# Sixteen sequences through four conditioned layers: modulation's columns at other places, softplus with Exp, Ln and a minimum, and the last attention with two score pairs and two weight buffers

## What is computed

```python
def _ssm(u, Wdbc, Wdt, bdt, Alog, Dp):            # E = 512, N = 16 states, R = 64
    dbc = einsum('bse,re->bsr', u, Wdbc)
    dlt, Bm, Cm = split(dbc, [R, R + N], axis=-1)
    delta = softplus(einsum('bsr,er->bse', dlt, Wdt) + bdt)
    dA = exp(delta[..., None] * -exp(Alog))
    dBu = delta[..., None] * Bm[:, :, None, :] * u[..., None]
    h = dA_t * h + dBu_t;  y = einsum('ben,bn->be', h, C_t)     # for each of 256 tokens
    return ys + u * Dp
# layer 0: shift, scale, gate = split(silu(c) @ Wada.T + bada)
#   xs = ln(x) * (1 + scale) + shift;  skip = xs;  xs = ln(xs)
#   mz = xs @ Wz + bz;  act_mx = silu(xs @ Wx + bx)
#   y = act_mx * ssm(mz @ Wc1, ...) + act_mx * flip(ssm(flip(mz @ Wc2), ...))
#   x = x + gate * (y @ Wf + bf + skip)
# layer 1: tokens permuted; xm, z = h @ W_in; causal convolution of 4, silu, the same state recurrence, * silu(z)
# layer 2: q, k, v for 16 heads of 16; att = softmax(q k^T) v; ln, modulation, silu, projection
# layer 3: q softmaxed over features, k over tokens, y = q (k^T v); ln, modulation, silu, projection
```

## Time and profile before

| | |
|---|---|
| median of 3 runs | 3309.78 us (3307.33 to 3313.04) |
| profiled execution, its own time | 3308.65 us |
| its span | 3306.9 us |
| mean granted TensorE clock | 0.979 of full speed |
| PE / weight load | 3026.8 / 2529.6 us busy |
| ACT / DVE / POOL | 2872.9 / 2686.5 / 2661.3 us busy |

### The profile page before, as it was taken

One profiled execution on the slowest core, in us unless ns is written; L12 is line 12 of the kernel. 1 busy time (PEld: TensorE's weight loads), 2 busy tenths in 40 slices (PEclk: granted clock), 3 DMA queues, 4 the chain that ended last, 5 costly groups with the idle time before them and its releaser, 6 DMA issues.

```text
span 3306.9 us, 63710 instructions
## 1 busy us (share of the span) xinstructions
PE 3026.8 (92%) x21772; PEld 2529.6 (76%) x21772; DVE 2686.5 (81%) x3433; ACT 2872.9 (87%) x6598; POOL 2661.3 (80%) x3086
## 2 busy tenths in 40 slices
PE   7768788999999999999999999999999999988886
PEld 4656667888887888888787888888788877777754
DVE  1577788979798988979798988979898988877752
ACT  2778879899999999999999999999999989887843
POOL 0596999989898988988898898989898888767720
PEclk8799999999999999999999999999999999999988
DMA  5122222222222222222222222222222121212200
GB/s 201 42 71 63 72 80 74 83 65 84 67 85 69 73 81 68 86 65 84 69 81 71 71 85 64 86 67 84 67 81 75 64 83 63 70 54 65 61 14 9
DMA packets 133873, 239.58 MB, mean 72 GB/s; under 512 B 15374, under 2 KB 31054, under 8 KB 133296
## 3 DMA queue, kind: packets, MB, share of 16 engines
q1 hardware_dynamic: 133552, 235.50, 23.1%
HBM read 230.36 MB, written 5.08 MB: 71 GB/s over the span
## 4 chain that ended last, share of the span: by engine, by line
PE 59%; ACT 13%; DVE 13%; issue 4%; POOL 4%; DVEq 0%; POOLq 0%; ACTq 0%
PE ps_b L697 13%; PE ps_y L725 12%; DVE hst L805 7%; PE ps_v L904 6%; ACT decay L764 5%; PE ps_x L1463 4%; PE ps_x L910 4%; POOL g L820 3%; PE ps_x L1437 3%; ACT dbut L775 2%; PE ps_x L904 2%; PE ps_v L955 2%; PE ps_v L910 2%; PE ps_x L1473 2%; POOL dbut L785 1%
## 5 line engine op out<-in xcount | busy, mean ns | idle before, releaser
L820 POOL TENSOR_TENSOR g<-hst,c_bc 128x512 f32<-128x512 f32 x1536 | 1980.3, 1290 | 405.9 <-PE ps_y L725 351.4
L805 DVE TENSOR_TENSOR_SCAN hst<-decay,ps_b 128x512 f32<-128x512 f32 x1536 | 1819.8, 1208 | 307.6 <-PE ps_b L697 160.3
L764 ACT ACTIVATE decay<-delta,acoef 128x256 f32<-128x256 f32 x3072 | 1377.7, 498 | 23.0 <-DVE hst L805 21.8
L697 PE MATMUL ps_b<-ident,dbut 128*128 128x128 f32 x6144 | 937.8, 276 | 158.4 <-DVE hst L805 71.9
L725 PE MATMUL ps_y<-ident,g 128*128 128x128 f32 x6144 | 936.5, 275 | 15.8 <-ACT u L1119 12.4
L697 PEld LDWEIGHTS ps_b<-ident,dbut 128*128 128x128 f32 x6144 | 702.2, 142 | 235.6 <-issue 133.0
L785 POOL TENSOR_SCALAR dbut<-dut,bcm 128x256 f32<-128x256 f32 x1536 | 753.5, 491 | 97.1 <-ACT dut L1018 97.1
L725 PEld LDWEIGHTS ps_y<-ident,g 128*128 128x128 f32 x6144 | 725.9, 141 | 138.1 <-issue 59.2
L775 ACT ACTIVATE dbut<-dut,bcm 128x256 f32<-128x256 f32 x1536 | 766.4, 500 | 30.3 <-PE ps_b L697 28.2
L1518 ACT ACTIVATE pT<-ps_x 128x1024 f32<-128x1024 f32 x120 | 121.5, 1012 | 39.5 <-PE ps_x L1473 26.9
L1546 DVE TENSOR_REDUCE mxt<-ps_x 128x4 f32<-128x1024 f32 x120 | 144.5, 1204 | 8.7 <-PE ps_x L1437 8.7
(11 more groups left out here) (257 smaller groups left out, 3711.5 us busy)
## 6 DMA issues: line engine op xcount, KB each, us to landing
...
```

What stands on the lines that cost most here:

```text
L697: last = nc.tensor.matmul(ps_b[:, u % 2, e * T + t * P:e * T + (t + 1) * P], dbut[:, u % NDBU, t, e * P:(e + 1) * P], ident[:, :], is_tran ...
L764: last = nc.scalar.activation(decay[:, u % (DA_AHEAD + 2), e, :], delta[slot(b, s)][:, eb, :], ACT.Exp, scale=acoef[:, s, eb, n:n + 1])
L805: nc.vector.tensor_tensor_scan(line(hst[:, u % NHST, :, :].rearrange("p e t -> p (e t)")), line(decay[:, u % (DA_AHEAD + 2), :, :].rearran ...
L820: nc.gpsimd.tensor_tensor(g[:, u % NG, :, :], hst[:, u % NHST, :, :], c_bc[:, k % NCB * CHUNK + n % CHUNK, :].unsqueeze(1) .broadcast_to([ ...
```

## The change

1. `ada` gets other places, (64, 65, 94.5, 106.182 to 106.955) for PE and 111 for DVE, after `BASE[0]` = 112: three pieces within the first sequence's scans, nine in the hole at ticks 218 and 219 where the first sequence's last scans and the second's first meet. What needs its columns in stage 1 (`l1_in` and others) moves a few ticks.
2. Softplus: Abs is gone, Exp reads PSUM; Ln(1 + Exp) as before; DVE takes max(min(that, 44), value). So each half has one ACT instruction less, six for a sequence, and the pieces of `prep` on ACT are 10 in place of 12.
3. `ps_y` becomes the first bank of `ps_v`, which has three; the other two keep their use.
4. `Attention` has lists `pairs` and `weights`. `late` has the pairs `ps_b` and `ps_v`, and the weights `pT` and two buffers of `g`; score group g waits for g - 2, and Exp for g - 2.
5. Pieces of the steady part and of the special stages get new places. In the start, prep1, mx and silu of the first sequence, formerly spread over ticks 107 to 123, are at ticks 122 and 123.

```diff
+LN_TOP = 44.0
...
-Attention = namedtuple("Attention", "pair pv xt q k v y")
+Attention = namedtuple("Attention", "pairs weights pv xt q k v y")
...
     "prep1": {
-        "PE": (46, 48, 66, 69, 78, 92, 95, 96),
-        "ACT": (61, 67, 72, 72, 76, 79, 80, 80, 95, 95, 95, 96),
+        "PE": (46, 48, 66, 69, 78, 92, 94, 95),
+        "ACT": (61, 67, 72, 76, 79, 80, 92.875, 94, 94.875, 95),
         "DVE": (78, 82, 90),
...
         "prep1": {
-            "PE": (107, 107, 111.25, 112, 117, 120, 122, 123),
-            "ACT": (112, 114, 114.333, 114.5, 114.667, 117.5, 117.75, 118, 120.667, 121, 122, 123),
-            "DVE": (116, 119, 120),
+            "PE": (111, 112, 122.091, 122.273, 122.455, 122.818, 122.909, 123),
+            "ACT": (122, 122.071, 122.143, 122.214, 122.357, 122.429, 122.714, 122.786, 122.857, 123),
+            "DVE": (123, 123, 123),
...
         "ada": {
-            "PE": (-112.824, -112.765, -112.647, -112.529, -112.471, -112.412, -112.353, -112.294, -112.235, -112.118, -112.059, -112),
-            "DVE": (-5.6,),
+            "PE": (64, 65, 94.5, 106.182, 106.227, 106.455, 106.591, 106.636, 106.773, 106.818, 106.864, 106.955),
+            "DVE": (111,),
         },
...
         "l2_tail": {
-            "PE": (24, 28, 28, 29),
+            "PE": (24, 27, 27, 28),
...
         ps_b = ps("ps_b", [P, 2, 512])
-        ps_y = ps("ps_y", [P, TB, HALF * P])
-        ps_v = ps("ps_v", [P, 2, 512])
+        ps_v = ps("ps_v", [P, 3, 512])
+        ps_y = ps_v[:, 0, :].rearrange("p (t n) -> p t n", t=TB)
         ps_x = ps("ps_x", [P, 3, 512])
-        A, B_ = 0, 1
+        A, B_ = 1, 2
...
                 d = delta[i][:, 2 * k:2 * k + 2, :]
-                ch.done(nc.scalar.activation(d, bank(ps_v, v, 2), ACT.Abs))
-                yield next(at)
                 logexp()
-                ch.done(nc.scalar.activation(d, d, ACT.Exp, scale=-1.0))
+                ch.done(nc.scalar.activation(d, bank(ps_v, v, 2), ACT.Exp))
...
-                nc.vector.scalar_tensor_tensor(out=d, in0=bank(ps_v, v, 2), scalar=0.0, in1=d, op0=ALU.max,
-                                               op1=ALU.add).then_inc(S[f"dt_read_{s}"], 1)
+                nc.vector.scalar_tensor_tensor(out=d, in0=d, scalar=LN_TOP, in1=bank(ps_v, v, 2), op0=ALU.min,
+                                               op1=ALU.max).then_inc(S[f"dt_read_{s}"], 1)
...
-                else:
-                    pe.wait_ge(S["s_max"], nth("s_max", b, g_))
+                elif g_ >= len(a.pairs):
+                    pe.wait_ge(S["s_max"], nth("s_max", b, g_ - len(a.pairs) + 1))
+                pair = a.pairs[g_ % len(a.pairs)]
...
-                    else:
-                        pe.wait_ge(S["p_ready"], nth("p_ready", b, g_))
+                    elif g_ >= len(a.pairs):
+                        pe.wait_ge(S["p_ready"], nth("p_ready", b, g_ - len(a.pairs) + 1))
...
-                if g_ >= 1:
-                    act.wait_ge(S["o_full_2"], nth("o_full_2", b, g_))
+                if g_ >= len(a.weights):
+                    act.wait_ge(S["o_full_2"], nth("o_full_2", b, g_ - len(a.weights) + 1))
...
-        usual = Attention(ps_x, (ps_x, 2), xt_x, qT, kT, v2, yv)
-        late = Attention(ps_b, (ps_v, B_), dbut[:, 0, :, :], decay[:, 0:2, :, :].rearrange("p a e t -> p (a e) t"),
+        usual = Attention([ps_x], [pT[:, :, :, :]], (ps_x, 2), xt_x, qT, kT, v2, yv)
+        late = Attention([ps_b, ps_v], [pT[:, :, :, :], g[:, 0:2, :, :]], (ps_v, B_), dbut[:, 0, :, :], decay[:, 0:2, :, :].rearrange("p a e t -> p (a e) t"),
```

301 lines of the change are left out of this document (158 added, 143 removed).

## The result

The changed kernel takes 3289.86 us (median of 4 runs, 3288.62 to 3297.11), the kernel before 3308.99 us on the same chip: ratio 0.9943, interval 0.993 to 0.9955. It is 19 us faster. The forecast was 44 us less, down to 3265; the time lies at the very end of the range. Six more runs of the same kernel gave 3286.51 (3280.41 to 3294.19), ratio 0.9934, 0.9922 to 0.9947. The profiled execution is the slowest of its four, 3297.11 us; where it lost the time is part of what follows.

A forecast was written before the change was run, and what follows sets the result against it. PE was taken to pace most of the kernel, ACT some. Start -11, second hole -1, softplus -21 and tail -11 sum to -44 us against 3308.65: forecast 3265 us, range 3238 to 3290.

The forecast's parts named there:

- Softplus: In the preps, six Abs per period leave ACT, 3.55 us; 1.6 taken as gain, -21 us in 13 periods.
- an Abs at the head of a stretch as in the earlier trace: ACT chain between 1690 and 1710 us, Abs at 1699.39: such an Abs was held worth its 0.6 us in full.
- steady gains nothing: Rival for the steady periods: Abs always lay beside PE, so removing it gains nothing; 3285.7 us, chance 0.17.
- The start: Up to the first scan: modulation moved out, first scan 16 us earlier, 4.7 given back; net -11 us, bounds -16 and -5.
- The 3.2 us behind the product: In the start, mx's projections and half of the second dbc projection come after the first transposes: another 3.2 us gained.
- the one gap of 12 us: Among the first 16 scans, prep1, silu and mx in one place: 12 us lost instead of 7.3, +4.7.
- The second hole: Hole of sequence 1: takes 36 of 48 modulation matmuls, 4.2 us of PE, two Abs leave; -1 us, between -2 and +3.
- The tail: Last sequence's end: scores -9, second half -3, end -1, x2's later start +2; sum -11 us, between -4 and -20.
- The rival on the clock of the start: Transposes leave PE at 1.2 GHz through the first units and the hole: 3.8 us slower than forecast, 3269 us, chance 0.10.
- The stall in each period: Rival: prep1's second transposes, one unit earlier in PE's queue, wait for ACT's copy; up to 3.9 us per period, 3337, chance 0.06.
- the moved places: Pieces moved one tick here and there, and ps_y now a bank of ps_v: costed at nothing, covered by slack.

The follow-up runs named there:

- ada_back: The changed kernel with the modulation back before the first scan, all else as in the change: 3305.05 us (12 runs), ratio 0.9986 to the kernel before.
- change_again: The changed kernel, unedited, run once more: 3286.51 us (six runs), its profiled execution 3282.86 us.
- ada_spread: The changed kernel with the modulation's 12 pieces one to each fourth unit of the first sequence's scans, DVE's behind them: 3291.66 us (5 runs), ratio 0.9948.

## Why the prediction was right or wrong

**Softplus: the step that failed.** "But Abs sits where ACT is densest, in preps. I take 1.6 of 3.55, in 13 periods -21." Measured: 0.0 per period, and 1.0003 for the part alone. Half the forecast was this term. What failed is the overlap: 1.6 us of each 3.55 were taken as standing alone, and all of it stood beside other work. It should have been read per slice: each of the six Abs stands in a slice where ACT isn't full or another engine is too, which the windows of the kernel before showed. The sentence that an Abs at the head of a stretch as in the earlier trace rows is worth its 0.6 in full fell with it: that Abs is the sixth of its period, the one in the slice from 1502.83 where PE is full, and leaving it out gave nothing. That ACT's rows lie on one of several chains of about equal length would explain why the chain's share was no price; it was not shown. The rival "steady gains nothing", at 3285.7 with a chance of 0.17, is what happened: 3289.9 and 3286.5.

**The start: right in mechanism, its sizes a little small.** The product was expected at 84.1 and came at 79.69, the first scan 20.4 us earlier and not 16; ada_back gives 18.5 us to the modulation's place alone. The first half had waited behind modulation matmuls as well, which the sum left out: its projection for delta started at 75.82 before and at 71.43 now. The 3.2 us behind the product were 3.1. In place of the one gap of 12 us there were two, of 11.4 and 8.3 from scan to scan, and the lead at unit 24 was 14.2: 6.2 given back in place of 4.7, 7.2 in change_again.

**The second hole: wrong.** "-1, between -2 and +3": it grew by 4.5 us. The range's reason, modulation matmuls on PE, was wrong too, since the hole is 16.9 without them; what the term left out is the new order of the other projections in PE's queue, read from the traces at ada_back. Part of it came back: change_again was 12.3 ahead at unit 72, 7.9 at unit 76, 12.3 again at unit 84 and 11.0 at unit 120; the profiled execution after had 12.4, 7.9, 10.3 and 8.2.

**The tail: right.** -9 for the scores (measured -10.5), -3 for the second half (-1.8), -1 at the end (-1.3), +2 for x2's later start (it leaves 3.9 us later against the last scan, and the scores start 3.7 later); in sum -11 against -9.9, in other executions of the same tail up to -16.7. The clock did rise, 0.65 to 0.74 here and to 1.00 in ada_spread, where I had kept it nearly as it was: by the clock alone these eight groups take from 13.84 to 17.33 us.

**What luck did.** Without the softplus term the prediction stands at 3285.7, close to 3286.5 and 3289.9. That is in part a balance: the start gave 2 to 3 us more than forecast, the second hole took 2 to 5 more, and the steady part took 2 that were put at nothing.

**The rival on the clock of the start** fell. From the first units on PE had mostly transposes (and the projection of dbc at L946, two matmuls at a time, among them), at 0.50 until 92.06, some 4.5 us into the scans, where the sum had full clock. The four windows, all of the profile after:

```profile
81.00:90.00 9.00, 6.15 (x23) 4.62 (x24) 3.39 (x7) 7.76 (x19) 2.88 (x5) 0.50 0.00 0
90.00:96.00 6.00, 5.39 (x36) 4.51 (x35) 5.20 (x5) 6.00 (x16) 6.00 (x9) 0.83 0.14 48
119.36:126.19 6.83, 4.54 (x20) 4.14 (x21) 4.15 (x10) 5.81 (x16) 1.73 (x2) 0.50 0.01 2
126.19:136.00 9.81, 9.56 (x72) 8.84 (x71) 6.76 (x6) 9.80 (x26) 9.42 (x11) 1.00 0.16 58
```

In the second of these windows all but the end of one such projection are transposes of 128x128, and the granted clock went up to its upper level, 2.4 GHz (mean 0.83). Four matmuls of that projection had run just before, so the third window is the cleaner one: PE's 20 instructions in it are transposes of 128x128 without exception, at 0.50, and at its end the clock went up and stayed up in the fourth. The Trainium skill's sentence that the full clock does not engage for transposes ("TensorE: Matmul & The Clock Gate", Part 4: PE-mode transpose) does not hold here. What the rival had right is that the clock was low at times: 0.50 up to 92.06, and again from 119.36 to 126.19, in the second of the two gaps, after PE had been idle for 4.90 us.

**The stall in each period** did not come either: the period is 187.0 as before. But the moved places, put at nothing, with ps_y's new bank cost 2.0 us over nine periods, and 0.0 where softplus alone was changed. Which of them it was, no run shows.

What stays open is which chain sets the 187.0 us of a period. ACT's busy time was cut by 3.4, 2.4 and 1.1 us at different places for 0.0 each, PE's by 1.8 for 0.8, both together by 2.2 (PE) and 3.8 (ACT) for 1.3. That several ladders of nearly one length run through it fits all of these; it was not shown for each.
